# Relative attention's position scores written to HBM in rows that begin and end on 64-byte lines

## The reference, cut to what matters

```python
B, S, D, H, P = 32, 512, 256, 16, 16          # batches, tokens, width, heads, width of a head
q, k, val = heads(xn @ Wq + bq), heads(xn @ Wk + bk), heads(xn @ Wv + bv)
pos = (sinusoid(S, D) @ Wp + bp)              # [H, S, P]
content_score = einsum('bhsp,bhtp->bhst', q + u, k)
pos_score = einsum('bhsp,htp->bhst', q + v, pos)

def _relative_shift(x):                       # x: [b, h, s, s]
    x = jnp.pad(x, ((0, 0), (0, 0), (0, 0), (1, 0)))   # a zero ahead of each row: s x (s + 1)
    x = x.reshape(b, h, s + 1, s)             # the same numbers, read in rows of s
    return x[:, :, 1:, :].reshape(b, h, s, s)

score = (content_score + _relative_shift(pos_score)) / sqrt(P)
out = einsum('bhst,bhtp->bhsp', softmax(score), val)    # then @ Wo + bo
```

## Time and profile before

| | |
|---|---|
| time, median of 3 runs | 5464.18 us (5462.42 to 5471.35) |
| the profiled execution's own time | 5409.13 us |
| its span, first to last instruction | 5407.3 us |
| loop over the heads, first to last write L348 | 154.3 to 3451.3 us |
| TensorE busy | 5052.8 us (93%) |
| VectorE, ScalarE busy | 3619.1 us, 3459.4 us |
| writes L348 | 512 of 1026.0 KB, 10.4 us from issue to landing (median) |
| reads L356 | 512 of 1024.0 KB, 8.5 us |
| DMA, whole span | 1357.75 MB, 311142 packets |

### The profile page before, as it was taken

How to read it: one execution, slowest core, us unless ns; L and a number is a source line. 1 busy time by engine, 2 the same in 40 slices (tenths; PEclk the granted TensorE clock), 3 DMA queues, 4 the chain that set the end, 5 groups by cost and what they waited for, 6 DMA issues and landing times. The chain is left out here.

```text
span 5407.3 us, 126833 instructions
## 1 busy us (share of the span) xinstructions
PE 5052.8 (93%) x42412; PEld 3753.5 (69%) x42412; DVE 3619.1 (67%) x8008; ACT 3459.4 (64%) x5116; POOL 1429.7 (26%) x1032
## 2 busy tenths in 40 slices
PE   7899999999999999999999999899999999999755
PEld 3566666666666666666666666588888898898744
DVE  7699988888888788788888888743333333333233
ACT  3688888888888788788788888643444444344211
POOL 0112111111111111111111121134444444444365
PEclk9799999999999999999999999999999999999888
DMA  9899999999999999999999999853223222322398
GB/s 346 314 341 335 330 338 341 334 343 336 339 338 330 338 342 330 332 344 333 334 343 334 336 341 353 276 169 58 52 52 58 50 53 56 60 43 44 80 305 263
DMA packets 311142, 1357.75 MB, mean 251 GB/s; under 512 B 41792, under 2 KB 119360, under 8 KB 179136
## 3 DMA queue, kind: packets, MB, share of 16 engines
q1 hardware_dynamic: 256704, 1265.12, 68.2%
q0 software_dynamic: 49152, 67.14, 7.6%
q10 hardware_dynamic: 4608, 16.78, 0.8%
HBM read 691.42 MB, written 657.46 MB: 249 GB/s over the span
## 5 line engine op out<-in xcount | busy, mean ns | idle before, releaser
L677 DVE CUSTOM_DVE_ANT_0 att_shifted<-att_quad,att_shifted 128x512 f32<-128x512 f32 x2048 | 1330.3, 683 | 248.5 <-PE att_quad L921 162.5
L542 ACT ACTIVATE att_shifted<-att_shifted,att_mn 128x512 f32<-128x512 f32 x2048 | 1359.5, 717 | 71.7 <-issue 65.4
L537 ACT ACTIVATE att_xo<-att_quad 128x1024 f32<-128x1024 f32 x1024 | 1048.3, 1024 | 500.5 <-PE att_quad L909 500.1
L942 PE MATMUL att_tp<-att_ident,att_shifted 128*128 128x128 f32 x8192 | 1142.5, 283 | 0.9 <-ACT att_shifted L542 0.4
L687 DVE COPY att_pt<-att_tp 128x512 f32<-128x512 f32 x1536 | 1011.3, 685 | 194.8 <-PE att_tp L942 193.9
L942 PEld LDWEIGHTS att_tp<-att_ident,att_shifted 128*128 128x128 f32 x8192 | 894.9, 143 | 304.7 <-issue 281.8
L1255 DVE TENSOR_TENSOR ffn_hp<-ffn_hf,ffn_hp 128x512 fp32r<-128x512 f32 x512 | 354.9, 693 | 926.0 <-ACT ffn_hf L1222 925.9
L1220 ACT ACTIVATE ffn_hp<-ffn_up 128x512 fp32r<-128x512 f32 x512 | 305.9, 597 | 927.1 <-PE ffn_up L1312 927.0
L909 PE MATMUL att_quad<-att_pos,att_qv 64*128 64x512 f32 x2048 | 852.8, 455 | 17.4 <-ACT att_xo L537 17.4
L1286 PE MATMUL ffn_yp<-ffn_w2p,ffn_hp 128*128 128x256 f32 x6144 | 830.1, 285 | 28.9 <-DVE ffn_w2p L1263 22.8
L1286 PEld LDWEIGHTS ffn_yp<-ffn_w2p,ffn_hp 128*128 128x128 f32 x6144 | 806.6, 193 | 69.4 <-issue 29.2
(11 more groups left out here) (108 smaller groups left out, 4966.4 us busy)
## 6 DMA issues: line engine op xcount, KB each, us to landing
xs_d<-att_xo SPq DMA_DIRECT2D x512, 1026.0 KB, 10.4
att_shifted<-xs_d SPq DMA_DIRECT2D x512, 1024.0 KB, 8.5
att_shifted<-in_L_attn_x_dram SPq DMA_DIRECT2D x32, 512.0 KB, 7.1
xn_d<-att_shifted SPq DMA_DIRECT2D x32, 512.0 KB, 6.4
xt_d<-att_shifted SPq DMA_DIRECT2D x32, 512.0 KB, 7.6
att_xf<-xt_d SPq DMA_DIRECT2D x32, 512.0 KB, 9.1
att_d<-att_osb SPq DMA_DIRECT2D x512, 32.0 KB
ffn_d<-ffn_zero SPq DMA_DIRECT2D x8, 2048.0 KB, 24.8
```

The lines of the kernel that those rows point to most:

```text
L537: act.activation(xo[:, kk % NW, 2 * half:2 * half + 2, 1:S + 1], xp[:, :, :], ACT.Copy).then_inc(x_out, 1)
L542: act.activation(shifted[:, kk % NX, t], shifted[:, kk % NX, t], ACT.Exp, bias=mn[:, kk % NX, t:t + 1], scale=-1.0).then_inc(exp_done, 1)
L677: dve.tensor_tensor_reduce(out=shifted[:, kk % NX, t], in0=sp_[:, t % 2], in1=shifted[:, kk % NX, t], scale=-0.25, scalar=-NEG, op0=ALU.ad ...
L942: ins = pe.transpose(tp[:, c % 2, t * P:(t + 1) * P], shifted[:, kk % NX, t, c * P:(c + 1) * P], ident[:, :])
```

## The change

Each DMA piece now covers whole 64-byte lines of HBM. Partition p of `xo` gets room for 12 words (EDGE) more behind its 2052. After ScalarE's two copies, a DMA from SBUF to SBUF (`copy_edge`) brings the first 12 words of partition p + 1 there, for p = 0 to 126. Then `write_x` writes the head with four DMAs, one for each remainder r of the partition's number modulo 4, of 32 pieces each. A piece begins at the first line that begins in its own 2052 words and goes on to the end of the line in which they end: 8256 bytes for r = 0 and 8192 bytes for the other three. The same bytes as before arrive in HBM, each once. `write_x` waits for its edge's landing (`x_edged`, a semaphore for each buffer) in place of `x_out`. `x_written` now rises by 64 for a head, and `read_x` and `x_evacuate` wait for that.

LEAD goes from 5 to 6, so TensorE and ScalarE make the positions one head further ahead. In step kk SyncE now issues the edge of head kk + 5, the four writes of head kk + 4 and the read of head kk + 3, in this order. The buffers stay NW = 4 and NX = 8. In the prologue, positions 4 and 5 are made behind `spread_qu(0, 0)`, and the writes and reads begin one head later against the copies.

```diff
-    LEAD = 5
+    LEAD = 6
+    LINE = 16
+    ROW = TT * (S + 1)
+    EDGE = LINE - TT
...
-        xo = m.sb("xo", [P, NW, TT, S + 1])
+        xo = m.sb("xo", [P, NW, ROW + EDGE])
...
+                def copy_edge(i, kk):
+
+                    wait_alone(sp, x_out, (i * BH + kk + 1) * 2)
+                    buf = kk % NW
+                    sp.dma_start(xo[0:P - 1, buf, ROW:ROW + EDGE], xo[1:P, buf, 0:EDGE]).then_inc(x_edged[buf], 16)
+
                 def write_x(i, kk):
 
                     slot, turn = of_slot(kk)
-                    wait_alone(sp, x_out, (i * BH + kk + 1) * 2)
+                    buf = kk % NW
+                    wait_alone(sp, x_edged[buf], (i * (BH // NW) + kk // NW + 1) * 16)
 
                     wait_alone(sp, x_shifted[slot], (i * (BH // NX) + turn) * 16)
-                    sp.dma_start(xs_d[slot].rearrange("(p t c) -> p t c", t=TT, c=S + 1), xo[:, kk % NW]).then_inc(x_written[slot], 16)
+                    rows = xs_d[slot].rearrange("(m n) -> m n", n=LINE // TT * ROW)
+                    for r in range(LINE // TT):
+                        begin, end = -r * TT % LINE, ROW + -(r + 1) * TT % LINE
+                        sp.dma_start(rows[:, r * ROW + begin:r * ROW + end], xo[r:P:LINE // TT, buf, begin:end]).then_inc(x_written[slot], 16)
...
-                    wait_alone(sp, x_written[slot], (i * (BH // NX) + turn + 1) * 16)
+                    wait_alone(sp, x_written[slot], (i * (BH // NX) + turn + 1) * (LINE // TT * 16))
...
                     for kk in range(BH):
                         if not (last and kk + LEAD - 1 >= BH):
-                            write_x(i, kk + LEAD - 1)
+                            copy_edge(i, kk + LEAD - 1)
                         if not (last and kk + LEAD - 2 >= BH):
-                            read_x(i, kk + LEAD - 2)
+                            write_x(i, kk + LEAD - 2)
+                        if not (last and kk + LEAD - 3 >= BH):
+                            read_x(i, kk + LEAD - 3)
...
-                for t in range(TT):
-                    position(0, 4, t)
                 pe.wait_ge(kd_out, 1)
                 spread_qu(0, 0)
+                for k in range(4, LEAD):
+                    for t in range(TT):
+                        position(0, k, t)
```

More of the change, by code:

```diff
@@ L245, in attention_phase @@
         x_out = m.sem("x_out")
+        x_edged = [m.sem(f"x_edged{k}") for k in range(NW)]
         x_written = [m.sem(f"x_written{k}") for k in range(NX)]
@@ L372, in _ @@
                 for k in range(LEAD - 1):
-                    write_x(0, k)
-                    if k == 2:
+                    copy_edge(0, k)
+                    if k:
+                        write_x(0, k - 1)
+                    if k == 3:
                         for n in range(NS):
@@ L377, in _ @@
                             sp.wait_ge(xt_stored[n], 16 * (B // NS))
-                    if k:
-                        read_x(0, k - 1)
+                    if k > 1:
+                        read_x(0, k - 2)
                 load_xt(1)
@@ L405, in _ @@
                 pool.memset(val[:, :, :, :, HD:HD + 1], 1.0).then_inc(ones_set, 1)
-                pool.memset(xo[:, :, :, 0:1], 0.0).then_inc(edge_set, 1)
+                pool.memset(xo[:, :, 0:ROW].rearrange("p k (t c) -> p k t c", t=TT)[:, :, :, 0:1], 0.0).then_inc(edge_set, 1)
                 def in_order(tile):
@@ L534, in x_evacuate @@
                         slot, turn = of_slot(kk - NW)
-                        act.wait_ge(x_written[slot], (i * (BH // NX) + turn + 1) * 16)
+                        act.wait_ge(x_written[slot], (i * (BH // NX) + turn + 1) * (LINE // TT * 16))
                     act.wait_ge(x_full, (i * BH + kk) * 2 + half + 1)
-                    act.activation(xo[:, kk % NW, 2 * half:2 * half + 2, 1:S + 1], xp[:, :, :], ACT.Copy).then_inc(x_out, 1)
+                    act.activation(xo[:, kk % NW, 0:ROW].rearrange("p (t c) -> p t c", t=TT)[:, 2 * half:2 * half + 2, 1:S + 1], xp[:, :, :], ACT.Copy).then_inc(x_out, 1)
                 def exponential(i, kk, t):
@@ L560, in _ @@
                 act.wait_ge(edge_set, 1)
-                for k in range(LEAD - 1):
+                for k in range(NW):
                     x_evacuate(0, k, 0)
@@ L568, in _ @@
                 act.activation(p3, p3, ACT.Exp).then_inc(exped, 1)
-                x_evacuate(0, LEAD - 1, 0)
-                x_evacuate(0, LEAD - 1, 1)
+                for k in range(NW, LEAD):
+                    x_evacuate(0, k, 0)
+                    x_evacuate(0, k, 1)
                 keep_queries(0, 1)
```

## The result

The changed kernel took 6256.87 us, median of 4 runs (6250.13 to 6265.1), against 5463.3 us for the kernel before (4 runs, 5443.56 to 5471.35). The ratio is 1.1459, with a 95% interval of 1.1426 to 1.1493. The direction was forecast, the size was not: the forecast was 5794 us, and its upper end of 6230 us is passed by 27 us. The profiled execution after has a span of 6253.2 us, 845.9 us more than the one before (5407.3 us).

What follows compares the result with a forecast made beforehand. TensorE was taken to bound the loop, DMA right behind. One engine carrying every edge would lengthen the period from 6.463 to 7.12 us; over 500 heads 330 us, so 5464 + 330 = 5794 us, range 5400 to 6230 us.

Steps and rivals of the forecast that it cites:

- What bounds: Loop over heads: TensorE sets the 6.463 us pace, DMA right behind with 6.33 us of work per head.
- The edge on one engine: Edge copy: all 127 pieces run on one engine, 10.3 ns each, 1.31 us of engine time per head.
- The sum: Loaded engine per head: 5.77 us data, 1.31 edge, 0.04 completions make 7.12 us, the new period.
- Relief: Four aligned writes: a head's data takes 5.77 us of DMA; ends 5.34 (full relief) and 6.33 us (none).
- SyncE's list: Issues per head grow from 1.9 to 3.3 us, covered by 2.6 us of waiting; costed at nothing.
- LEAD = 6, costed at nothing: Copies come one head sooner, so writes and reads keep their distance to VectorE's `add`; no cost entered.
- The wait for the edge: SyncE's wait `x_edged`: edge issued one step earlier, some 5 us ahead, so no cost.
- the buffer's shorter return: Reuse of `xo`: 17.3 of about 21 us taken, 4 us left, so costed at nothing.
- A hidden edge: Rival in the loop: edge spread or cheap, lines bring relief, TensorE alone bounds; 5392 to 5400 us, chance 0.13.
- no change: Rival: relief and edge cancel, or the read's lateness stays; 5464 us, chance 0.07.
- the strided source: Rival: write pieces from partitions 4 apart slow each other in SBUF; 8.6 us per head, 6510 us, chance 0.12.
- the sign that I gave for it: Sign of slower writes from the strided source: loop's DMA share stays at 0.98 with fewer GB/s.

Runs made afterwards that it cites:

- e8: Kernel before with LEAD of 6 and SyncE's new order of steps, one unaligned write, no edge copy; ratio 1.0209.
- e2: Changed kernel without the edge copy and its wait, keeping four aligned writes and LEAD of 6; ratio 1.0256.
- e3: Kernel before with its one write cut into four strided, unaligned writes, LEAD of 5, no edge copy; ratio 0.9959.
- e9: Kernel before, LEAD of 5 and its old order, with four writes in whole 64-byte lines but no edge copy; ratio 0.9945.
- e10: Changed kernel without the edge copy, with content scores moved to the other 64 rows of TensorE; ratio 0.9931.
- e1: Changed kernel with edge copy and LEAD of 6, but each head written by one unaligned DMA of 128 pieces; ratio 1.1005.
- e6: Changed kernel with the full edge of 127 pieces issued from ScalarE's queue in place of SyncE's; ratio 1.0763.
- e17: Changed kernel with the edge cut into three DMAs of 43, 43 and 41 pieces, and one unaligned write; ratio 1.1217.
- e15: Changed kernel with an edge of 113 pieces in place of 127; ratio 1.0928.
- e11: Changed kernel, edge included, with content scores moved to the other 64 rows of TensorE; ratio 1.152.
- e12: Changed kernel with an edge of only 16 pieces, one for each engine, keeping its issue and wait; ratio 1.0329.
- e16: Changed kernel with the edge in two DMAs of 112 and 15 pieces, and one unaligned write; ratio 1.0449.

## Why the prediction was right or wrong

**What bounds.** Right: TensorE sets the pace and DMA comes right behind. LEAD = 6 showed the first (0.31 us more of TensorE per head and a period longer by 0.19 us in e8), the edge the second.

**The edge on one engine.** Right in kind and in count, not in price. Packets under 512 bytes grew by 72827 / 317 - 53.0 = 176.7 per head, where 176 were forecast for one engine and 191 for all. A piece took 11.0 ns by itself (forecast 10.3), but pieces overlap, and an edge took up its engine for 0.90 us, not 1.31. The share of 103.8% in the earlier trace rows was the sign that packet times there overlap as well and are no engine time.

**The sum, 7.12 us against 8.20 measured.** Its terms, from the trace after: work 6.27 less the edge's mean of 0.09 is 6.18 us of data and completions (forecast 5.81), edge 0.90 (1.31). That makes 7.08 us, by luck close to the forecast, since the two errors cancel. 1.12 us are left that no term has, 560 us over 500 heads. (Counted as the prediction did, with 1.40 for the edge, the terms make 7.58 us and 0.62 us are left.)

**Relief, the first mis-sized term.** Without an edge the four writes did bring DMA's work down to 5.85 to 5.94 us per head (e2, e3, e9, e10), near the 5.77 that I took. But cutting the write does it (6.37 to 5.94 in e3), not the lines (5.94 to 5.86 in e9). With the full edge in the queue half of it is lost again, 6.18 us, where the sum had 5.81. And since TensorE is the bound in those kernels, it shows in the time as 0.4 to 0.8%.

**SyncE's list, the term costed at nothing.** This is the step that failed. I priced an issue at 0.34 us from a DMA of 128 partitions, found 2.6 us of waiting per head as cover, and said that the queue had 10.8 us in hand. A write of 32 partitions takes 0.60 us to issue. And an issue is not a fixed price: held by the pieces that wait for the loaded engine it took up to 4 to 6 us. Even before the change the issues of L348 ran from 0.32 to 1.63 us in this stretch. So the list, put at 3.3 us, came to 6.85 us of issues per head, against 4.21 us in e2 without the edge. It lost its waiting, became full (no wait in the stretch), and what was in hand in the queue was gone with it: landing 5.2 us, and no packet under way for 0.38 us per head. Of this the prediction had only 1 us in one head of four; the steps with a `store_o` took 10.5 us from read to read and the others 7.4 us.

The part of it that the experiments show is 0.64 us per head: so much the four writes cost behind a full edge (8.20 after against 7.56 in e1), and only 0.08 us without one (e2 against e8). The rest is not assigned. Beyond the loaded engine's sum, with 0.90 us for the edge, the period of e1 is 0.30 us longer (7.56 for 7.26), that of e6 0.42 us (7.32 for 6.90), of e17 0.55 us (7.81 for 7.26) and of e15 0.63 us (7.54 for 6.91). In e1 no packet is under way for 0.06 us per head only, so some engine nearly always works; whether it is the loaded one, and on what, stays open.

**From which point the edge decides.** Between 61 pieces, which cost nothing, and 113, which cost 0.79 us per head over e2. No run lies between them. The engine's sum does not give the point: e2's work of 5.93 us leaves 0.82 us of its 6.75 us, room for 116 pieces at 7.06 ns.

**LEAD = 6, costed at nothing.** Wrong: 2.1% without the edge (e8, which e10 puts down to the halves). I asked what it does to distances in the queue and not which rows of TensorE the moved matmuls share. Behind the edge it is hidden (e11), so it had no part in the 14.6%.

**The wait for the edge and the buffer's shorter return, costed at nothing.** In the kernel after SyncE never waits for the edge: right. The return was not: ScalarE waits 499.1 us for writes. Alone the step costs 0.7% (e12) to 2.4% (e16).

**Rivals.** A hidden edge and no change are excluded by the result; the strided source by e3; and the sign that I gave for it (share at 0.98 with fewer GB/s) did not come, the share fell to 0.76. The checks on GB/s (267, forecast some 305), on the share and on VectorE's waits came in the right direction and beyond their size. That the measured time is close to the upper end is luck: that end has 6.33 us of data and an edge of 1.63 us in it, and the runs show 6.18 and 0.90 us. The range was too narrow because it was built from the engine's sum alone, and SyncE's list had been given no range.

## What to carry to other kernels

A DMA whose partition count has no large divisor (127) puts all its pieces on one engine: add the pieces to that engine's work, take the sum as a lower bound, and give 128 or 112 partitions where a divisor can be had. Price a small piece by the distance from start to start and not by its own duration, since pieces overlap. Treat the issuing queue as a resource with a range: when one engine has a backlog the issues behind it are held, and waiting time that looked like cover disappears; look at the minimum, median and maximum of the issues, and at whether the list still waits anywhere. When a software pipeline's distance changes by one, ask which buffers, banks and rows alternate by parity.

## What the hardware showed that I had not expected

- An issue takes as long as the queue lets it: 0.32 us for the 1026 KB write without an edge, 4.50 us in the median behind one (up to 6.28), while 127 pieces of 48 bytes lay on one engine. The hold ended 0.17 to 0.18 us behind the edge's first piece (e1, after). Landing times got shorter in the kernel after (10.8 to 5.2 us). Which store of the queue is full then is not settled.
- Pieces of 48 bytes from SBUF to SBUF took 11.0 ns each and started 7.06 ns apart on one engine, 127 of them in 0.90 us (after, e1, e11).
- A DMA of 32 partitions took 0.60 us to issue (e2, e3, e10), one of 128 partitions 0.32 us.
- Cutting a write of 1026 KB into four of 32 partitions each, 4 apart, lowered DMA's busy time per head from 6.37 to 5.94 us at the same bytes. Why is open; a busy record may include waiting. e8, with the write uncut, reads 6.29 us.
- Beginning and ending the pieces on 64-byte lines changed the time by less than the intervals (0.9945 against 0.9959; 0.9931 against 0.9917).
- Two matmuls of 64 rows start together on different halves and 0.23 to 0.33 us apart on the same half, worth 0.35 us per head of TensorE's time.
